# Both shared experts ahead of the routed experts in the last layer of a four-layer model

## The reference

```
topk_idx, topk_w = gate(x)             # 4 of 16 experts, sigmoid scores, groups of 4, 2 groups kept
g = x @ gate_proj[e].T;  u = x @ up_proj[e].T          # 256 -> 352, for the token's experts e
y = sum over its experts of  w_e * ((silu(g) * u) @ down_proj[e].T)
y = y + (silu(x @ shared_gate.T) * (x @ shared_up.T)) @ shared_down.T    # 256 -> 704 -> 256
out = x_residual + tanh(g_ffn[3]) * y
```

## Time and profile before

| | us |
|---|---|
| median of 3 runs | 2856.97 |
| lowest and highest run | 2855.2, 2863.26 |
| span of the profiled execution, first to last instruction | 2967.7 |
| PE, DVE, ACT, POOL busy in that span | 2448.3, 1310.7, 889.4, 661.7 |
| mean granted TensorE clock | 0.908 |

### The profile page before, as it was taken

The page is one execution under the profiler, slowest core; times in us unless marked ns, Lnnn a source line. Parts: engine busy times, 40 slices in busy tenths (PEclk is TensorE's granted clock), DMA queues, the critical chain, the costliest instruction groups (busy, mean ns, idle before and its releaser), DMA issues.

```text
span 2967.7 us, 32107 instructions
## 1 busy us (share of the span) xinstructions
PE 2448.3 (82%) x11498; PEld 1620.8 (55%) x11498; DVE 1310.7 (44%) x2761; ACT 889.4 (30%) x1980; POOL 661.7 (22%) x747
## 2 busy tenths in 40 slices
PE   6898888988798399977899799999883299999925
PEld 3455654555366177753446564446562168888703
DVE  6664366634565311116573536573536023333204
ACT  3453244623341022214553225562210011111100
POOL 3052230122022400013111310002202602222360
PEclk9999999998898599988999999999885699999967
DMA  9000000000002322200000000000002225555330
GB/s 360 22 1 1 1 1 1 1 1 0 8 1 111 142 93 95 92 32 18 11 15 1 1 1 1 1 1 0 1 1 96 103 70 199 199 199 199 133 97 28
DMA packets 64402, 173.28 MB, mean 58 GB/s; under 512 B 6608, under 2 KB 45136, under 8 KB 56208
## 3 DMA queue, kind: packets, MB, share of 16 engines
q0 software_dynamic: 21280, 95.11, 9.3%
q1 hardware_dynamic: 43008, 76.66, 7.2%
HBM read 121.81 MB, written 49.94 MB: 58 GB/s over the span
## 4 chain that ended last, share of the span: by engine, by line
PE 71%; DVE 14%; another core or an unknown queue 5%; issue 4%; ACT 4%; POOL 1%; DMA 0%; DVEq 0%; ACTq 0%; SPq 0%; POOLq 0%
PE PS L2201 8%; PE PS L982 6%; PE PS L973 6%; PE PS L576 6%; PE PS L1976 5%; PE PS L1990 5%; PE PS L2215 4%; PE PS L606 4%; PE PS L932 3%; PE PS L517 3%; PE PS L556 2%; PE PS L2116 2%; DVE arena L680 2%; PE PS L763 2%
## 5 line engine op out<-in xcount | busy, mean ns | idle before, releaser
L637 ACT ACTIVATE arena<-PS,arena 128x512 f32<-128x512 f32 (+3 forms) x512 | 306.4, 606 | 208.8 <-DVE arena L680 169.5
L680 DVE TENSOR_REDUCE arena<-PS 128x1 f32<-128x512 f32 (+3 forms) x512 | 273.0, 583 | 141.2 <-PE PS L582 85.0
L576 PE MATMUL PS<-arena 64*128 64x512 f32 (+3 forms) x1024 | 294.5, 567 | 31.2 <-ACT arena L637 20.0
L2201 PE MATMUL PS<-arena 128*128 128x256 f32 (+1 forms) x1128 | 252.1, 379 | 0.9 <-DVE arena L2239 0.9
L2201 PEld LDWEIGHTS PS<-arena 128*128 128x128 f32 (+1 forms) x1128 | 203.4, 180 | 40.7 <-issue 1.1
L288 POOL TENSOR_TENSOR arena<-arena 128x4 f32<-128x4 f32 x41 | 47.1, 1148 | 724.1 <-DVE arena L299 432.7
L2116 PE MATMUL PS<-arena 128*128 (+1 forms) x192 | 98.4, 668 | 116.0 <-issue 93.8
L606 PE MATMUL PS<-arena 128*128 128x128 f32 x1280 | 172.0, 279 | 17.7 <-ACT arena L637 12.8
L576 PEld LDWEIGHTS PS<-arena 64*128 64x128 f32 x1024 | 104.0, 187 | 144.3 <-ACT arena L637 94.3
L606 PEld LDWEIGHTS PS<-arena 128*128 128x128 f32 x1280 | 138.8, 142 | 72.6 <-ACT arena L637 45.0
L861 POOL TENSOR_TENSOR arena<-arena 128x512 f32<-128x512 f32 (+2 forms) x108 | 89.1, 828 | 382.3 <-ACT arena L832 376.6
(11 more groups left out here) (348 smaller groups left out, 3962.0 us busy)
## 6 DMA issues: line engine op xcount, KB each, us to landing
arena<-e SPq DMA_DIRECT2D x8, 2048.0 KB
arena<-slots SPq DMA_DIRECT2D x55, 256.0 KB, 2.7
yslots<-arena POOLq DMA_DIRECT2D x55, 256.0 KB, 7.8
slots<-zeros SPq DMA_DIRECT2D x1, 12032.0 KB, 40.2
slots<-zeros SPq DMA_DIRECT2D x1, 5120.0 KB, 35.1
arena<-w3a SPq DMA_DIRECT2D x1, 4106.0 KB, 13.6
arena<-w3b SPq DMA_DIRECT2D x1, 3593.0 KB, 21.8
arena<-slots SPq DMA_DIRECT2D x8, 384.0 KB, 8.8
```

The lines of the kernel that those rows point to most:

```text
L576: ins = nc.tensor.matmul(PS[:, hh, 0:w], q[:, t * P:(t + 1) * P], k[:, 0:w], start=True, stop=not cfg["causal"])
L637: nc.scalar.activation(PRB[m % 6][:, 0:w], PS[:, hh, 0:w], ACT.Exp, bias=nmax[:, m:m + 1], accum_out=rsum[:, col:col + 1]).then_inc(s["pro ...
L680: nc.vector.tensor_reduce(nmax[:, m:m + 1], PS[:, hh, 0:w], AX, ALU.max, negate=True).then_inc(s["nmax"], 1)
L2201: ins = nc.tensor.matmul(PS[0:n, 2 * c + up, 0:BN], wbuf3[i][:, off:off + n], xsT3[i][:, k, :], start=k == 0, stop=k == KC - 1)
```

## The change

On PE, ACT and DVE the call `shared3(1)` moves from behind `moe3` to right behind `shared3(0)`. The counts that the waits compare with follow from the new order: the steps of shared expert 1 no longer count the 47 batches ahead of them (`h0 = 0`), and the batches count both shared experts' steps (`SH`, `SO`). PE's wait of shared expert 1 for the outputs of all batches goes; PE's wait ahead of the first batch now asks for the accumulations of both shared experts. POOL's and SP's streams stay as they are.

```diff
         def pe_shared3(pe, i):
-            s, h0 = s3m, i * NB3 * 3
+            s, h0 = s3m, 0
             pe.wait_ge((s["wa"], s["wb"])[i], 16)
-            if i:
-                pe.wait_ge(s["copied"], NB3 + 3)
             with pe.Fori(0, B) as b:
...
-                dve_accumulate(v, s, it, b, i * NB3)
+                dve_accumulate(v, s, it, b, 0)
...
-        SH, SO = B * 3, B * QT
+        SH, SO = 2 * B * 3, 2 * B * QT
...
         def pe_moe3(pe):
             s = s3m
-            pe.wait_ge(s["acc"], 4 + NT)
+            pe.wait_ge(s["acc"], 4 + 2 * NT)
...
             pe_shared3(pe, 0)
+            pe_shared3(pe, 1)
             pe_moe3(pe)
-            pe_shared3(pe, 1)
...
             act_shared3(act, 0)
+            act_shared3(act, 1)
             act_moe3(act)
-            act_shared3(act, 1)
...
             dve_shared3(v, 0)
+            dve_shared3(v, 1)
             dve_moe3(v)
-            dve_shared3(v, 1)
             dve_combine3(v)
```

## The result

The changed kernel takes 2903.43 us (median of 4 runs, 2900.12 to 2904.69); the kernel before took 2858.09 us beside it (median of 4, 2855.2 to 2863.26). The ratio is 1.0151, 95% interval [1.0137, 1.0165], so 43 us (39 to 47) slower by the ratio (the two medians stand 45 apart); forecast were 2900 us and +42.8. But one thing in the prediction was wrong, and it has to be told first.

The account below looks back on a forecast made before the run. In timed runs the scatter bounds the front, and gathers and shared expert 1 together the tail; recorded delays are absent. Front +43.4 and tail -0.6 give +42.8 us on 2857.0: 2899.8, stated as 2900, range 2880 to 2922.

Parts of the forecast that it names:

- The front: Ahead of the batches: shared expert 1's steps start the first batch 46.5 us later, less 3.1 for PE's clock: +43.4.
- The tail: Behind the batches: shared expert 1's 64.3 us leave, but gathers alone take 95.3 us against 95.9: 0.6 us won.
- The clock: At the first batches: PE no longer idles for the scatter beforehand and so stays at full clock, saving 3.1 us.
- 2967.7 - 42.2 - 68.5 = 2857.0: Kernel before: recorded span less the delays' cost at the front and in the tail gives the timed median, 2857.0 us.
- the delay should still stand under the scatter: Changed kernel's profile: PE's late signals return in shared expert 0's second step, about 69 us; first batch near 2480.
- the span of 2963: Changed kernel's recorded span: about 2963 us, not longer than before, while the timed runs are 43 us slower.
- Rival A: PE's late signals under scatter and gathers occur in timed runs too: +64.3 and -69.1, net -4.8 us, 2852; chance 0.12.
- Rival B: PE's late signals occur in timed runs only under the gathers behind the batches: -25.7 us, 2831; chance 0.06.
- Rival C: Behind the batches: 48 weighted sums slow POOL's gather issues, the last gather 20 us later: 2920 us; chance 0.06.

Follow-up runs that it names:

- second recording of before: The kernel before, recorded again with no edit: 2858.19 us, ratio 1.0002, span 2857.0.
- Half of the scatter: The kernel before with 32 indirect writes in the scatter instead of 64: 2840.03 us, ratio 0.9935.
- the split of one step: Against the kernel before: one step of the shared experts ahead of the batches and seven behind, instead of four and four; ratio 1.0178.
- half of the gathers: 32 gathers and sums instead of 64, in both kernels: the kernel before 2843.48 us, ratio 0.9946; the changed kernel 2856.62 us, ratio 0.9995 to the kernel before.
- five ahead: Against the kernel before: five steps of the shared experts ahead of the batches and three behind, instead of four and four; ratio 0.9992.

## Why the prediction was right, and where it was not

The block starts at other times in different recordings (first step at 2282.19 us in the second recording of before, 2280.87 in that of the change, 2278.1 to 2285.6 in all nine), so each term is measured from a point within it.

| term | predicted | measured |
|---|---|---|
| before: first step to first batch | 86.0 | 86.9 (2282.19 to 2369.04) |
| after: first step to first batch | 132.5 | 132.8 (2280.87 to 2413.69) |
| what a cool PE costs the batches, first product to last copy | 3.1 | 3.0 (390.9 against 387.9) |
| before: last copy to end | 95.9 | 97.0 (2759.98 to 2856.99) |
| after: last copy to end | 95.3 | 96.6 (2801.59 to 2898.2) |
| sum | +42.8 | 46.0 - 3.0 - 0.4 = +42.5 |

- *The front* came out within 0.9 us: 64.3 us of steps were moved to where 18.4 us stood open. Half of the scatter (19 us) and the split of one step show the scatter as the front's bound before, and the changed kernel's loads, 47 us early, show that it no longer is.
- *The tail*: 64.3 us of work left and only 0.4 us came back, since the gathers cannot start before the last store. The two experiments with half of the gathers show both sides of that.
- *The clock*: the 3.1 us that PE wins back by not idling are there, to 0.1 us. The price does not follow the length of the idle time. From first product to last copy the batches take 3.0 us more than the change's 387.9 after 18.4 us of idle time, the same after 67 us (one ahead), and 1.5 more after 2.7 us (five ahead). With half of the scatter they take 1.7 more after waits of 0.6 and 0.9 us, for which the change itself pays nothing; what separates these two is not shown.
- *How the time of the runs was found*: the step "2967.7 - 42.2 - 68.5 = 2857.0" gave the before's undelayed span; the second recording has 2857.0. That it agrees to the tenth is luck: the block starts 2.0 us earlier there, front and tail are 0.9 and 1.1 us longer, and the 1.6 to 2.0 us by which an execution's time stands above its span were left out.
- *The failed step* is "the delay should still stand under the scatter" and the span of 2963 from it. The prediction put the delays down to recording. The runs showed them in one recorded execution and in none of the nine after it (the change and eight experiments), in all of which POOL issues the same two series of indirect DMAs, whole or by half, beside PE or alone: the changed kernel's first batch started at 2413.69, not near 2480, and its span was 2898.2, not 2963. That the timed runs lack the delays was right; why that one execution had them stays open. No run here brought them back.
- *Rival A* fell with the runs: +43, not -4.8. The odd recording's span stood 110.7 us above the median of the runs, while in the nine later ones the execution's time is 1.6 to 2.0 us above the span. The Trainium skill (Runtime: NRT & Kernel Launch, the preamble and postamble breakdown) gives a profile's total as some 6.2 us above the executed time. The span here goes from first to last instruction and is not that total, so no run here tests that figure, and the prediction's 110.7 us was not the quantity to set against it. *Rival B* would have been 2831.
- *Rival C*, sums that slow the gathers: in the changed kernel 48 sums run beside them, and from the first to the last of the 64 issues are 79.7 us; in the second recording of before, with some 46 sums beside them, 80.1. With one step ahead, where all sums come later, they are 78.9 (2767.7 to 2846.6), as in the earlier trace rows. That is 0.8 to 1.2 us where the rival priced 20.

```profile
L2319 POOL DMA_INDIRECT arena<-yslots,slot_of x64: 942/947/1142, 2805.2 to 2884.9; - x64
...
L2321 POOL DMA_INDIRECT arena<-yslots,slot_of x64: 942/946/1281, 2763.6 to 2843.7; - x64
```

The Trainium skill (SBUF — State Buffer, who interferes with whom) infers, for another DVE instruction with two SBUF inputs (tensor_tensor), that it takes only the read side of the port pair shared with GpSimd, while descriptor generation needs the write side. The sums' small price agrees with that.

## What to carry to other kernels

Before moving work, ask what runs beside it at the old place and what stands open at the new one: here 64 us of PE work were free under the gathers, and only 18 us were open under the scatter. When, as here, the span of a profile and the timed runs differ by 4%, don't read the profile as it stands: take out the waits that nothing explains, see whether the rest adds up to the runs, and record again. The best place for a block of work that two series could cover can be a split between them: here four or five steps ahead, which the runs can't tell apart.

## What the hardware did that I had not expected

In one execution ACT started up to 22 us after the PE records that it needed, while PE went on 0.05 us after ACT, under two series of 64 indirect DMAs, and in nine other recordings never. That PE's signals were late is read from these times, since the rows name only "remote" as releaser; DVE, which waits for PE's down projections, was late in that stretch too (its last two accumulations of the first step begin at 2306.72 and 2313.73, behind products that are through by 2301.9). And an idle time of 18.4 us costs PE 3.0 us behind it: granted 0.50 while it idled and 0.55 in the 8 us after. An idle time of 67 us cost the same.
